# First phase of a decoder kernel: x in whole 4 KB pieces three pairs ahead, rotation tables kept in the down matrix's place, query weights behind x

## The chip, the cores and the metric

The kernel runs on one core of a Trainium2 chip. The metric is the device time of one execution in microseconds, as the median of several runs. PE is the matrix engine, DVE the vector engine, ACT the scalar engine, POOL the general engine; SP only issues transfers.

## What is computed

x and a context are [16, 256, 512], float32. Three residual steps:

```
x = x + attention(layernorm(x))          # 16 heads of 32, one shared key and value head
x = x + wkv(keys = layernorm(x), values = context)     # a recurrence over the 256 steps
x = x + ffn(layernorm(x))                # gate, up, down with ternary weights, 8-bit activations
```

What makes a first phase necessary: in the attention K and V pass through a low-rank squeeze and are then quantised to 8 bits with the minimum and maximum over **all** batches,

```
K = rope(x @ wk.T) @ k_compress.T @ k_decompress.T ;  V = x @ wv.T @ v_compress.T @ v_decompress.T
q = clip(round((t - t.min()) / ((t.max() - t.min()) / 255)), 0, 255)       # t = K, and t = V
```

so no batch's attention can start before all 16 batches' keys and values are known. Queries are rotated (rope) and attend in windows of 128 with step 64, with a normalised sigmoid. In the ffn each of the three weight matrices (4 MB) is divided by the mean of its absolute values over the whole matrix and rounded to -1, 0, 1.

## The kernel before

Activations lie in HBM twice: `x` by rows, and `xT` transposed by the host, both [16, ...] per batch. Weights come transposed too.

**First phase**, over 8 pairs of batches (j). `sync_program` loads x of the pair (`load_x`, L260, one DMA of 512 KB a batch, in pieces of 2 KB) into one of two buffers, and xT (`load_columns`, pieces of 1 KB) into one of three. DVE takes row statistics (`keys_stats`), POOL the inverse deviations (`row_rstd`), PE projects xT with the centred key and value weights (`keys_project`, L429), spreads the deviations over partitions by transposing (`keys_spread`, L440), DVE multiplies the spread deviations with the rotation table (`keys_rope`, L905, into `rope_rows`, two buffers) and the projection with that (L912); PE then applies the low-rank matrices (`keys_grow`, L449 and L456). ACT copies the raw keys and values out and stores them to HBM scratch (`keep_raw`), DVE keeps the extremes (`keys_ext`, L917). SP stores the cosine and sine rows to scratch too (`store_trig`, L272), two pairs behind the loads and in the same in-order queue; DVE's next write of that buffer waits for the store. A load of x waits until the statistics of two pairs earlier are done, a load of columns for the projection three pairs earlier. The query weights `wq_sb` are loaded at pair 3, their column means taken by PE at pair 6 (L464), and DVE centres them there (`queries_centre`, L898). After pair 7 `set_grid` takes the extremes over all partitions, with a POOL reduction.

**Between.** SP's order after the last pair's loads: queries of batch 0, its keys, its residual rows, the stores of the last two pairs' tables, four chunks of gate weights into `work` (`load_weights`, L279), the context. ACT sums each chunk's absolute values (`sum_weights`, L685, `junk` is its discarded result); after the fourth, DVE and POOL make the mean (`weight_mean`, `weight_total`).

**The loop** is a software pipeline over the batches written out by hand: iteration i does the attention of batch i, the wkv step and ffn of earlier ones. In iteration 0 DVE's order is: `keys_grid(0)`, `rope(0, 0)`, `rope(0, 1)` (L1023), `weight_mean(GATE)`, `rotate(0, 0)` (L1029), then the gate rounding (`round_weights`) and `rotate(0, 1)`. `rope` waits for PE's query products (L494, two halves), `rotate` for a transfer that swaps neighbouring rows (`turn_queries`, L319); PE's scores (L513) wait for `rotate`, and ACT's sigmoid (L722) for those. Up and down weights are loaded, summed and rounded in iterations 0 to 2, each into the chunk of `work` that the one before has left.

Of the kernel before, what the change touches and what calls it, by code (L numbers as in the profile page):

```python
# [12 lines left out]
I = 2048  # L13
# [26 lines left out]
def build(nc, a, out, k_scratch, v_scratch):  # L40

    def sb(name, shape, dt=fp32):
# [4 lines left out]
    ident_bf = sb("ident_bf", [P, P], bf16)  # L47
# [101 lines left out]
    rope_rows = [small(3 * HD, 2 * S).rearrange("p (u s) -> p u s", u=2) for k in both]  # L149
    k_raw = [small(HD, 2 * S).rearrange("p (u n) -> p u n", u=2) for k in both]  # L150

    raw = [small(P, 2 * 2 * NT * HD).rearrange("p (g n e) -> p g n e", g=2, n=2 * NT) for k in both]
    v_raw = [raw[k][:, 1].rearrange("p (u t) e -> p u t e", u=2) for k in both]
# [4 lines left out]
    squeeze_T, grow_k, grow_v = small(2 * MLA, 3 * HD), small(2 * MLA, HD), small(2 * MLA, HD)  # L158
# [7 lines left out]

    def w_chunk(m, k):
        return work[:, k * I:(k + 1) * I]
# [18 lines left out]
    first_loads, large_loads = event("first_loads", 6, 16), event("large_loads", 2, 16)  # L187
    const_loads = event("const_loads", 5, 16)
    x_loaded = [[event(f"x_loaded{k}{u}", unit=16) for u in both] for k in both]
    x_in_loaded = [event(f"x_in_loaded{k}", 2, 16) for k in range(3)]  # L190
    trig_stored = [event(f"trig_stored{k}", 2, 16) for k in both]
    kv_stored = [event(f"kv_stored{k}", 3, 16) for k in both]
# [62 lines left out]
    def sync_program(sy):  # L255

        def load_x(j, u):
            if j >= 2:
                sy.wait_ge(key_bn.sem, key_bn.at(j - 2))
            sy.dma_start(x_in[j % 2][:, u], a["x"][2 * j + u].rearrange("(t p) d -> p t d", p=P)).then_inc(  # L260
                x_loaded[j % 2][u].sem, 16)

        def load_columns(j, u):
            if j >= 3:
                sy.wait_ge(key_kv.sem, key_kv.at(j - 3))
            sy.dma_start(xT_in[j % 3][:, u], a["xT"][2 * j + u].rearrange("(c p) s -> p c s", p=P)).then_inc(
                x_in_loaded[j % 3].sem, 16)

        def store_trig(j):
            sy.wait_ge(key_rows.sem, key_rows.at(j))  # L270
            for u in both:
                sy.dma_start(k_scratch[2 * j + u, :, S:].rearrange("e (n s) -> n e s", n=2),  # L272
                             rope_rows[j % 2][0:2 * HD, u, :]).then_inc(trig_stored[j % 2].sem, 16)

        def load_weights(m, k):
            if m:
                sy.wait_ge(w_tern[m - 1].sem, w_tern[m - 1].at(0, k))
            dst = w_chunk(m, k)
            sy.dma_start(dst.rearrange("p (c n) -> p c n", n=D) if m == DOWN else dst, mats[m][k]).then_inc(  # L279
                w_loaded[m][k].sem, 16)  # L280

        def load_residual(b):
            if b == 0:
                sy.wait_ge(key_bn.sem, key_bn.at(PAIRS - 2))
            if b >= 3:
                for t in range(NT):
                    sy.wait_ge(out_stored[t].sem, out_stored[t].at(b - 3))
            sy.dma_start(x_rows[b % 3], a["x"][b].rearrange("(t p) d -> p t d", p=P)).then_inc(res_loaded[b % 2].sem, 16)

        def load_queries(b):  # L290
            if b:
                sy.wait_ge(rotated.sem, rotated.at(b - 1))
            sy.dma_start(xT, a["xT"][b].rearrange("(c p) s -> p c s", p=P)).then_inc(xT_loaded.sem, 16)

        def load_keys(b):
            if b:
                sy.wait_ge(k_set.sem, k_set.at(b - 1))
                sy.wait_ge(v_set.sem, v_set.at(b - 1))
                sy.wait_ge(roped.sem, roped.at(b - 1))
            pair = b // 2  # L300
            sy.wait_ge(kv_stored[pair % 2].sem, kv_stored[pair % 2].at(pair // 2))
            sy.wait_ge(trig_stored[pair % 2].sem, trig_stored[pair % 2].at(pair // 2))
            sy.dma_start(kv_b[:, NW * HD:], k_scratch[b].unsqueeze(0).to_broadcast([QUAD, HD, 3 * S])).then_inc(
                kv_loaded.sem, 16)
# [52 lines left out]
        for j in range(PAIRS):  # L357
            for u in both:
                load_x(j, u)
                load_columns(j, u)  # L360
            if j >= 2:
                store_trig(j - 2)
            if j == 3:
                sy.dma_start(wq_sb[:, :, :], a["wqT"].rearrange("(c p) n -> p c n", p=P)).then_inc(wq_loaded.sem, 16)
        load_queries(0)
        load_keys(0)
        load_residual(0)
        for j in (PAIRS - 2, PAIRS - 1):
            store_trig(j)
        for k in range(NC):  # L370
            load_weights(GATE, k)
# [48 lines left out]
    def tensor_program(te):  # L420
# [13 lines left out]
        def keys_spread(j):  # L434
            st, mv, rs = stats["x"]
            te.wait_ge(key_rstd.sem, key_rstd.at(j))
            if j >= 2:
# [35 lines left out]
        for j in range(PAIRS + 1):  # L473
# [7 lines left out]
            if j == PAIRS - 2:  # L481
# [174 lines left out]
    def scalar_program(se):  # L656

        se.dma_start(wkv_sb, a["wkvT"].rearrange("(c p) n -> p c n", p=P)).then_inc(first_loads.sem, 16)
        for dst, src in ((squeeze_T, "squeeze_T"), (grow_k, "grow_k"), (grow_v, "grow_v"), (ident[:, :], "ident"),
                         (rope_kv, "rope_kv")):  # L660
            se.dma_start(dst, a[src]).then_inc(first_loads.sem, 16)

        def keep_raw(j):
            if j >= 2:
                se.wait_ge(kv_stored[j % 2].sem, kv_stored[j % 2].at(j // 2 - 1))
                se.wait_ge(key_ext.sem, key_ext.at(j - 2))
            se.wait_ge(key_grown.sem, key_grown.at(j, 0))
            se.copy(k_raw[j % 2], in_bank(6, 2)[0:HD]).then_inc(key_raw.sem, 1)
            se.wait_ge(key_raw.sem, key_raw.at(j, 0))
            se.dma_start(k_scratch[2 * j:2 * j + 2, :, 0:S].rearrange("u p n -> p u n"), k_raw[j % 2]).then_inc(  # L670
                kv_stored[j % 2].sem, 16)
            se.wait_ge(key_grown.sem, key_grown.at(j, 1))
            grown = bank[TOK_BANK[j % 2]][:, 0:4 * 2 * HD].rearrange("p (n g e) -> p g n e", n=4, g=2)
            se.copy(raw[j % 2], grown).then_inc(key_raw.sem, 1)
            se.wait_ge(key_raw.sem, key_raw.at(j))
            for u in both:
                se.dma_start(v_scratch[2 * j + u].rearrange("(t p) e -> p t e", p=P), v_raw[j % 2][:, u]).then_inc(
                    kv_stored[j % 2].sem, 16)
# [34 lines left out]
        def probs(b, c):  # L713
            for j in range(QUAD):
                if b and c == 0 and j == 0:
                    se.wait_ge(num_made.sem, num_made.at(b - 1))
                elif c == 0 and j == 0:
                    for k in both:
                        se.wait_ge(trig_stored[k].sem, trig_stored[k].at(PAIRS // 2 - 1))
                        se.wait_ge(kv_stored[k].sem, kv_stored[k].at(PAIRS // 2 - 1))  # L720
# [146 lines left out]
    def vector_program(ve):  # L867
# [6 lines left out]
        def keys_stats(j):  # L874
            st, mv, rs = stats["x"]
            if j:
                ve.wait_ge(key_mv.sem, key_mv.at(j - 1))
            for u in both:
                ve.wait_ge(x_loaded[j % 2][u].sem, x_loaded[j % 2][u].at(j // 2))
                for t in range(NT):  # L880
                    ve.bn_stats(st[:, NT * u + t, :], x_in[j % 2][:, u, t, :]).then_inc(key_bn.sem, 1)
# [19 lines left out]
        def keys_rope(j):  # L901
            ve.wait_ge(key_spread.sem, key_spread.at(j))
            if j >= 2:
                ve.wait_ge(trig_stored[j % 2].sem, trig_stored[j % 2].at(j // 2 - 1))
            ve.tensor_tensor(rope_rows[j % 2], in_bank(2 + j % 2, 2)[0:3 * HD],  # L905
# [6 lines left out]
            ve.tensor_tensor(roped_kv[j % 2], in_bank(4 + j % 2, 2)[0:3 * HD], rope_rows[j % 2], op=ALU.mult).then_inc(  # L912
                key_roped.sem, 1)

        def keys_ext(j):
            ve.wait_ge(key_raw.sem, key_raw.at(j))
            ve.tensor_reduce(ext[:, :, 0, 4 * j:4 * j + 4], raw[j % 2], AX.X, ALU.max).then_inc(key_ext.sem, 1)  # L917
            ve.tensor_reduce(ext[:, :, 1, 4 * j:4 * j + 4], raw[j % 2], AX.X, ALU.min, negate=True).then_inc(
                key_ext.sem, 1)

        def round_weights(m, k):
# [7 lines left out]
            ve.wait_ge(w_bound[m].sem, w_bound[m].at(0, k))  # L929
            ve.tensor_scalar(tern_dst[m][:, k, :], w_chunk(m, k), MAGIC, None, ALU.subtract).then_inc(  # L930
# [49 lines left out]
        for j in range(PAIRS + 1):  # L980
# [8 lines left out]
            if j == PAIRS - 2:  # L989
                queries_centre()  # L990
# [306 lines left out]
    def pool_program(ge):  # L1297
        for dst, src in ((ident_bf, "ident_bf"), (blend, "blend"), (wu, "wu")):
# [130 lines left out]
def tables():  # L1429
# [11 lines left out]
        "ident_bf": np.eye(P).astype(mybir.dt.np(bf16)),  # L1441
# [43 lines left out]
```

## Time and profile before

| | us |
|---|---|
| median of 3 runs (1102.84 to 1103.45) | 1103.22 |
| the profiled execution's own time | 1107.51 |
| its span, first to last instruction | 1106.2 |
| busy PE / DVE / ACT / POOL | 860 / 848 / 707 / 437 |

Times of instructions are counted from the span's start. PE and DVE are busy 78% and 77% of the span. "Slices" are 40 equal parts of it, 27.7 us each; the first phase and iteration 0 fill the first five. In the transfers' digits 9 is 90% or more of the 16 DMA engines busy; the clock column is the share of the full TensorE clock (2.4 GHz) that was granted.

### The profile page before, as it was taken

What the parts mean: (1) busy time and instruction counts of PE and PEld (TensorE: products, weight loads), DVE (VectorE), ACT (ScalarE), POOL (GpSimd) and SP (SyncE); (2) the same over time, 40 slices, a digit from 0 to 9 for tenths busy, and PEclk for the clock granted to TensorE, in tenths of its full rate; (3) what the DMA queues carried; (4) which work ended last, traced back from release to release, by engine and by line L of the source; (5) the groups of instructions that cost most, each with busy time, mean ns of one, the idle gap of its engine ahead of it and who ended that gap; (6) DMA issues with size and microseconds to landing.
All of it is one profiled execution on the core that took longest, in us unless ns stands there. A gap on an engine that the chain in (4) does not pass through costs nothing.

```text
span 1106.2 us, 21992 instructions
## 1 busy us (share of the span) xinstructions
PE 860.3 (78%) x8301; PEld 512.9 (46%) x8388; DVE 848.1 (77%) x1630; ACT 706.9 (64%) x1179; POOL 436.7 (39%) x495
## 2 busy tenths in 40 slices
PE   5782565768888889897988888888888888986655
PEld 2341444444455555555545555555555554543222
DVE  4552659798888888888888888888788888887953
ACT  0113838077777777777768686868586868594633
POOL 2110113225353535353535354544444444445532
PEclk9896786769999999999999999999999999998978
DMA  8867516011524252525242424243342525122132
GB/s 293 288 217 277 188 58 189 10 59 36 93 68 83 78 83 78 84 78 83 79 83 78 80 82 77 85 75 87 62 99 58 104 58 103 49 78 29 39 58 66
DMA packets 148762, 106.93 MB, mean 97 GB/s; under 512 B 99792, under 2 KB 126128, under 8 KB 147504
## 3 DMA queue, kind: packets, MB, share of 16 engines
q1 hardware_dynamic: 142128, 101.48, 36.2%
q0 software_dynamic: 656, 2.63, 0.7%
q10 hardware_dynamic: 5872, 1.42, 0.6%
q8 instruction: 66, 1.08, 0.4%
q14 instruction: 40, 0.33, 0.1%
HBM read 65.65 MB, written 10.49 MB: 69 GB/s over the span
## 4 chain that ended last, share of the span: by engine, by line
ACT 31%; PE 23%; DVE 18%; issue 15%; DMA 3%; SPq 2%; POOL 1%; DVEq 0%; ACTq 0%; POOLq 0%
PE bank L494 9%; ACT arena L722 6%; PE bank L593 5%; PE bank L513 5%; ACT L774 3%; ACT sums L729 3%; DVE junk L1146 3%; PE bank L583 2%; ACT sums L734 2%; ACT junk L774 2%; ACT junk L779 2%; DVE amax L1112 2%; DVE fs L1155 2%; ACT L745 2%; ACT L722 2%
## 5 line engine op out<-in xcount | busy, mean ns | idle before, releaser
L583 PE MATMUL bank<-w_up_gate,qT 128*128 128x512 bf16 x966 | 232.5, 386 | 48.4 <-ACT junk L774 24.1
L1350 POOL TENSOR_TENSOR work<-junk,lnw 128x512 f32<-128x512 f32 x128 | 188.2, 1490 | 125.1 <-DVE junk L1146 110.7
L1333 POOL TENSOR_TENSOR sums<-sums,blend 128x448 f32<-128x448 f32 x64 | 73.2, 1163 | 270.5 <-ACT sums L734 270.5
L583 PEld LDWEIGHTS bank<-w_up_gate,qT 128*128 128x128 bf16 x1024 | 96.5, 99 | 155.3 <-ACT junk L774 26.9
L593 PE MATMUL bank<-w_down,work 128*128 128x512 bf16 x483 | 125.6, 408 | 25.3 <-ACT junk L774 10.6
L494 PE MATMUL bank<-wide,wq_sb 128*128 128x256 f32 x512 | 117.7, 389 | 27.7 <-DVE rows L1047 27.7
L513 PE MATMUL bank<-wide,k_win 32*128 32x128 f32 x1536 | 70.5, 320 | 82.2 <-ACT arena L722 54.2
L722 ACT ACTIVATE arena<-bank 128x384 f32<-128x384 f32 x256 | 104.8, 496 | 36.7 <-PE bank L513 36.6
L494 PEld LDWEIGHTS bank<-wide,wq_sb 128*128 128x128 f32 x512 | 98.3, 195 | 53.1 <-issue 39.7
L774 ACT ACTIVATE junk<-bank,deq 128x512 f32<-128x512 f32 x128 | 86.3, 686 | 52.5 <-PE bank L583 50.7
L545 PE MATMUL bank<-wo_sb,wide 128*128 128x512 f32 x256 | 115.9, 607 | 4.1 <-DVE wide L1040 4.1
L1146 DVE TENSOR_TENSOR junk<-bank,junk 128x512 f32<-128x512 f32 x128 | 87.7, 685 | 28.4 <-PE bank L583 18.7
L513 PEld LDWEIGHTS bank<-wide,k_win 32*128 32x128 f32 x1536 | 56.7, 213 | 106.4 <-ACT arena L722 71.9
L758 ACT ACTIVATE work<-work,fs 128x2048 f32<-128x2048 f32 x32 | 63.9, 1996 | 58.8 <-DVE fs L1168 58.8
L1068 DVE TENSOR_TENSOR_SCAN sums<-wkv_s,sums 128x256 f32<-128x256 f32 x128 | 98.6, 838 | 0.0
L779 ACT ACTIVATE junk<-junk 128x512 f32<-128x512 f32 x128 | 80.7, 631 | 20.9 <-DVE junk L1146 20.8
L593 PEld LDWEIGHTS bank<-w_down,work 128*128 128x128 bf16 x512 | 48.3, 103 | 88.4 <-issue 25.6
L545 PEld LDWEIGHTS bank<-wo_sb,wide 128*128 128x128 f32 x256 | 49.7, 195 | 62.0 <-issue 55.7
L1155 DVE TENSOR_REDUCE fs<-work 128x1 f32<-128x2048 f32 x32 | 72.8, 2276 | 0.4 <-POOL work L1350 0.4
L1023 DVE TENSOR_TENSOR wide<-bank,kv_b 128x512 f32<-128x512 f32 x64 | 41.0, 683 | 39.8 <-PE bank L555 38.5
L752 ACT ACTIVATE wide<-wide,amax 128x512 f32<-128x512 f32 x32 | 21.4, 714 | 78.4 <-DVE amax L1124 78.4
L524 PE MATMUL bank<-arena,v_win 128*32 128x128 f32 x1536 | 55.6, 278 | 9.2 <-ACT sums L729 7.5
(150 smaller groups left out, 1541.2 us busy)
## 6 DMA issues: line engine op xcount, KB each, us to landing
rows<-in_x SPq DMA_DIRECT2D x24, 512.0 KB, 5.4
sums<-in_xT SPq DMA_DIRECT2D x16, 512.0 KB, 8.8
wide<-in_xT SPq DMA_DIRECT2D x16, 512.0 KB, 4.2
ctx_T<-in_ctxT SPq DMA_DIRECT2D x16, 512.0 KB, 4.0
wide<-wide SPq DMA_DIRECT2D x64, 128.0 KB, 2.1
out<-rows SPq DMA_DIRECT2D x32, 256.0 KB, 2.2
kv_b<-k_raw SPq DMA_DIRECT2D x16, 384.0 KB
wide<-in_x SPq DMA_DIRECT2D x8, 512.0 KB, 9.3
```

What stands on the lines that cost most here:

```text
L494: last = te.matmul(in_bank(k, 2)[:, n % 2, :], wq_sb[:, c, n * P:(n + 1) * P], xT[:, c, :], start=c == 0, stop=c == NC - 1)
L513: last = te.matmul(bank[j][:, n * P:(n + 1) * P], k_win[head, window], q_cos[head, c, window], start=True, stop=True, skip_group_check=True)
L545: last = te.matmul(bank[t][:, :], heads_T[:, c, t * P:(t + 1) * P], wo_sb[:, c, :], start=c == 0, stop=c == NC - 1)
L583: last = te.matmul(bank[4 + k % 4][:, :], qT[:, c, t * P:(t + 1) * P], w_up_gate[:, m, c, cols], start=c == 0, stop=c == NC - 1)
L593: last = te.matmul(bank[6 + t][:, :], hid_T[:, t, c, :], w_down[:, c, :], start=c == 0, stop=c == NI - 1)
L722: se.activation(prob[:, :, QUAD * c + j, :], bank[j][:, 0:NW * P].rearrange("p (k q) -> p k q", k=NW), ACT.Sigmoid, scale=float(1.0 / np.s ...
L774: se.activation(gated[:, n % 2, :], bank[4 + 2 * (n % 2)][:, :], ACT.Silu, scale=deq[:, 0, t:t + 1]).then_inc(silu_set.sem, 1)
L779: se.activation(gated[:, n % 2, :], hid[:, n % 2, :], ACT.Square, accum_out=fs[:, t, n:n + 1]).then_inc(sq_set.sem, 1)
L1068: ve.tensor_tensor_scan(state[:, c, n, 1:S + 1], sc["decay"][:, c:c + 1].to_broadcast([P, S]), GG[:, c, n, :], 0.0, ALU.mult, ALU.add).the ...
L1146: ve.tensor_tensor(hid[:, n % 2, :], bank[4 + k % 4][:, :], gated[:, n % 2, :], op=ALU.mult).then_inc(hid_set.sem, 1)
L1155: ve.tensor_reduce(col[t]["am"], hid_w[:, t, :], AX.X, ALU.max, apply_absolute_value=True).then_inc(h_peak.sem, 1)
L1350: ge.tensor_tensor(hid_w[:, t, cols], hid[:, n % 2, :], lnw[:, cols], op=ALU.mult).then_inc(z_set.sem, 1)
```

## The change

- x and xT (and the context) are laid out by the host so that each partition's part is one run of 4 KB; one DMA of 1 MB loads a pair's x, another its columns. The loop's loads use the same layout.
- x has three buffers; the third is chunk 2 of `work`. So gate chunk 2 waits for the statistics of pair 5.
- `rope_rows` has one place for every pair, in the memory of `w_down`; its stores go out three pairs behind, and the last three are placed between later loads. The down rounding waits for all of them.
- raw keys and values have four buffers in place of two; a pair's values are stored by one DMA.
- `wq` is loaded after all x, its means are taken at pair 7 ahead of that pair's `keys_grow`, and centred inside `set_grid`. The gate chunks are issued before the last three table stores, residual and context after them. `wo` and `lnw` are issued after the gate weights' total.
- PE's first work waits for two small loads in place of six (three of them joined into one, two with their own event); SP waits for those two after issuing pair 0. The unused `ident_bf` goes.

```diff
+    def w_chunk(m, k):
+        return work[:, k * I:(k + 1) * I]
-    x_in = [rows[:, 0:2], wide[:, 1:3, :].rearrange("p u (t d) -> p u t d", t=NT)]
+    x_in = [home.rearrange("p (u t d) -> p u t d", u=2, t=NT) for home in
+            (rows[:, 0:2].rearrange("p k t d -> p (k t d)"), wide[:, 1:3, :].rearrange("p k n -> p (k n)"),
+             w_chunk(0, 2))]
+    rope_rows = [w_down[0:3 * HD].rearrange("p c n -> p (c n)").bitcast(fp32)[:, j * 2 * S:(j + 1) * 2 * S].rearrange(
+        "p (u s) -> p u s", u=2) for j in range(B // 2)]
...
-        def load_x(j, u):
-            if j >= 2:
-                sy.wait_ge(key_bn.sem, key_bn.at(j - 2))
-            sy.dma_start(x_in[j % 2][:, u], a["x"][2 * j + u].rearrange("(t p) d -> p t d", p=P)).then_inc(
-                x_loaded[j % 2][u].sem, 16)
+        def load_x(j):
+            if j >= 3:
+                sy.wait_ge(key_bn.sem, key_bn.at(j - 3))
+            sy.dma_start(x_in[j % 3].rearrange("p u t d -> p u (t d)"), a["x"][2 * j:2 * j + 2].rearrange(
+                "u p n -> p u n")).then_inc(x_loaded[j % 3].sem, 16)
...
         def store_trig(j):
             sy.wait_ge(key_rows.sem, key_rows.at(j))
+            if j >= 4:
+                sy.wait_ge(trig_stored[j % 4].sem, trig_stored[j % 4].at(j // 4 - 1))
...
         def load_weights(m, k):
             if m:
                 sy.wait_ge(w_tern[m - 1].sem, w_tern[m - 1].at(0, k))
+            elif k == 2:
+                sy.wait_ge(key_bn.sem, key_bn.at(5))
...
         for j in range(PAIRS):
-            for u in both:
-                load_x(j, u)
-                load_columns(j, u)
-            if j >= 2:
-                store_trig(j - 2)
-            if j == 3:
-                sy.dma_start(wq_sb[:, :, :], a["wqT"].rearrange("(c p) n -> p c n", p=P)).then_inc(wq_loaded.sem, 16)
+            load_x(j)
+            load_columns(j)
+            if j == 0:
+                sy.wait_ge(first_loads.sem, first_loads.at(0))
+            if j >= 3:
+                store_trig(j - 3)
+        sy.dma_start(wq_sb[:, :, :], a["wqT"].rearrange("(c p) n -> p c n", p=P)).then_inc(wq_loaded.sem, 16)
         load_queries(0)
         load_keys(0)
+        load_weights(GATE, 0)
+        load_weights(GATE, 1)
+        store_trig(5)
+        load_weights(GATE, 2)
+        load_weights(GATE, 3)
+        store_trig(6)
         load_residual(0)
-        for j in (PAIRS - 2, PAIRS - 1):
-            store_trig(j)
-        for k in range(NC):
-            load_weights(GATE, k)
+        store_trig(7)
         load_values(0)
...
-            if j == PAIRS - 2:
+            if j == PAIRS - 1:
                 te.wait_ge(wq_loaded.sem, wq_loaded.at(0))
                 column_means(bank[0][:, :], wq_sb, wq_mean)
...
             ve.wait_ge(key_ext.sem, key_ext.at(PAIRS - 1))
             ve.tensor_reduce(ext1[:, :], ext[:, :, :, :].rearrange("p g m n -> p (g m) n"), AX.X, ALU.max).then_inc(ext_col.sem, 1)
+            queries_centre()
             ve.wait_ge(ext_everywhere.sem, ext_everywhere.at(0))
...
+        weight_total(GATE)
         ge.dma_start(wo_sb[:, :, :], a["woT"].rearrange("(c p) n -> p c n", p=P)).then_inc(large_loads.sem, 16)
         ge.dma_start(lnw[:, :], a["lnw"].to_broadcast([P, I])).then_inc(large_loads.sem, 16)
-        ge.wait_ge(key_kv.sem, key_kv.at(PAIRS - 1))
-        weight_total(GATE)
```

## Rows read from the trace of the kernel before

**Rows 1.** The page's transfers, by slices of 27.7 us, in tenths
```profile
DMA  8867516011524252525242424243342525122132
```
**Rows 2.** Chain of waits that ended last: start us, us, what
```profile
84.26 18.14 DMA work<-in_wgT
...
106.21 1.90 ACT junk L685 x2
...
108.13 0.17 DVE abs_sum L957
...
109.18 0.68 DVE wide L1029
...
110.00 1.71 PE bank L513 x24
```
**Rows 3.** Stretches: length, busy us of PE, PEld, DVE, ACT, POOL, clock, DMA share, GB/s
```profile
2.00:14.00 12.00, 2.10 (x9) 1.96 (x10) 0.07 (x1) 1.28 (x1) 2.27 (x5) 1.00 1.03 328
34.00:42.00 8.00, 6.12 (x22) 2.79 (x22) 4.35 (x19) 1.25 (x4) 1.21 (x2) 1.00 1.06 365
66.00:82.00 16.00, 15.43 (x61) 7.85 (x60) 9.62 (x20) 2.84 (x6) 1.21 (x2) 1.00 0.54 154
90.00:98.00 8.00, 0.00 (x0) 0.00 (x0) 0.00 (x0) 0.80 (x1) 0.00 (x0) 0.63 1.02 424
151.00:153.00 2.00, 2.00 (x11) 1.77 (x10) 0.81 (x5) 0.00 (x0) 0.94 (x2) 1.00 1.03 397
106.00:126.00 20.00, 8.95 (x144) 7.62 (x148) 16.66 (x19) 12.89 (x23) 0.40 (x1) 0.50 0.52 153
```
**Rows 4.** Waits of the engines, 0 to 100 us: total us, times, longest
```profile
DVE stats_x L881 <- DMA wide<-in_x: 10.1, 6, 2.3
...
DVE stats_x L881 <- DMA rows<-in_x: 9.1, 5, 3.3
...
PE bank L429 <- DMA sums<-in_xT: 9.1, 3, 5.4
```
**Rows 5.** Waits of SP's queue, 0 to 200 us
```profile
SPq L260 <- DVE stats_x L881: 19.7, 10, 9.8
```
**Rows 6.** PE in order of time, 14 to 29 us: start, us, what
```profile
14.63 6.47 PE L429 MATMUL bank<-sums,arena 128*96 128x512 f32 x8
...
21.38 3.60 PE L429 MATMUL bank<-sums,arena 128*96 128x512 f32 x8
...
27.26 1.91 PE L429 MATMUL bank<-sums,arena 128*96 128x512 f32 x4
```
**Rows 7.** Instructions in order of time, 60 to 180 us
```profile
68.94 3.65 PE L464 MATMUL bank<-wq_sb,arena 128*128 128x512 f32 x8
...
72.43 3.60 PE L429 MATMUL bank<-sums,arena 128*96 128x512 f32 x8
...
73.86 2.27 DVE L898 TENSOR_TENSOR wq_sb<-wq_sb,bank 128x2048 f32<-128x2048 f32 x1
...
80.93 7.13 PE L494 MATMUL bank<-wide,wq_sb 128*128 128x256 f32 x32
...
82.34 0.29 DVE L967 TENSOR_REDUCE ext<-ext 128x4 f32<-128x128 f32 x1
...
88.17 1.29 DVE L1023 TENSOR_TENSOR wide<-bank,kv_b 128x512 f32<-128x512 f32 x2 [1.30 <-PE bank L494]
...
110.00 1.66 PE L513 MATMUL bank<-wide,k_win 32*128 32x128 f32 x24 [21.94 <-DVE wide L1029]
```
**Rows 8.** The page's transfers by line: KB each, us from issue to landing
```profile
wide<-wide SPq DMA_DIRECT2D x64, 128.0 KB, 2.1
...
arena<-in_wkvT ACTq DMA_DIRECT2D x1, 192.0 KB, 4.6
```
**Rows 9.** Waits in the loop, 300 to 1000 us
```profile
PE bank L494 <- DVE rows L1047: 20.1, 12, 1.9
```
**Rows 10.** PE in order of time in the loop, 330 to 365 us
```profile
344.08 0.95 PE L513 MATMUL bank<-wide,k_win 32*128 32x128 f32 x24
```

More of the change, by code:

```diff
@@ L46, in build @@
     ident = sb("ident", [P, P])
-    ident_bf = sb("ident_bf", [P, P], bf16)
     blend = sb("blend", [P, OUTS])
@@ L148, in build @@
     roped_kv = [small(3 * HD, 2 * S).rearrange("p (u s) -> p u s", u=2) for k in both]
[L149 to L153, printed above, removed]
+    k_raw = [small(HD, 2 * S).rearrange("p (u n) -> p u n", u=2) for k in range(4)]
+    raw = [small(P, 2 * 2 * NT * HD).rearrange("p (g n e) -> p g n e", g=2, n=2 * NT) for k in range(4)]
+    v_raw = [raw[k][:, 1] for k in range(4)]
     wkv_sb = small(P, NC * 3 * HD).rearrange("p (c n) -> p c n", c=NC)
@@ L157, in build @@
     grown_by = small(3 * HD, 2 * HD)
-    squeeze_T, grow_k, grow_v = small(2 * MLA, 3 * HD), small(2 * MLA, HD), small(2 * MLA, HD)
+    low_rank = small(2 * MLA, 5 * HD)
+    squeeze_T, grow_k, grow_v = low_rank[:, 0:3 * HD], low_rank[:, 3 * HD:4 * HD], low_rank[:, 4 * HD:]
     mats = [a["wgT"].rearrange("(c p) n -> c p n", p=P), a["wuT"].rearrange("(c p) n -> c p n", p=P),
@@ L184, in event @@
         return Event(nc, name, per, unit)
[L187 to L192, printed above, removed]
+    first_loads, table_loads, large_loads = event("first_loads", 2, 16), event("table_loads", 2, 16), event("large_loads", 2, 16)
+    const_loads = event("const_loads", 4, 16)
+    x_loaded = [event(f"x_loaded{k}", unit=16) for k in range(3)]
+    x_in_loaded = [event(f"x_in_loaded{k}", unit=16) for k in range(3)]
+    trig_stored = [event(f"trig_stored{k}", 2, 16) for k in range(4)]
+    kv_stored = [event(f"kv_stored{k}", 2, 16) for k in range(4)]
     w_loaded = [[event(f"w_loaded{m}{k}", unit=16) for k in range(NC)] for m in range(3)]
@@ L300, in load_keys @@
             pair = b // 2
-            sy.wait_ge(kv_stored[pair % 2].sem, kv_stored[pair % 2].at(pair // 2))
-            sy.wait_ge(trig_stored[pair % 2].sem, trig_stored[pair % 2].at(pair // 2))
+            sy.wait_ge(kv_stored[pair % 4].sem, kv_stored[pair % 4].at(pair // 4))
+            sy.wait_ge(trig_stored[pair % 4].sem, trig_stored[pair % 4].at(pair // 4))
             sy.dma_start(kv_b[:, NW * HD:], k_scratch[b].unsqueeze(0).to_broadcast([QUAD, HD, 3 * S])).then_inc(
@@ L658, in scalar_program @@
         se.dma_start(wkv_sb, a["wkvT"].rearrange("(c p) n -> p c n", p=P)).then_inc(first_loads.sem, 16)
-        for dst, src in ((squeeze_T, "squeeze_T"), (grow_k, "grow_k"), (grow_v, "grow_v"), (ident[:, :], "ident"),
-                         (rope_kv, "rope_kv")):
-            se.dma_start(dst, a[src]).then_inc(first_loads.sem, 16)
+        se.dma_start(low_rank, a["low_rank"]).then_inc(first_loads.sem, 16)
+        for dst, src in ((ident[:, :], "ident"), (rope_kv, "rope_kv")):
+            se.dma_start(dst, a[src]).then_inc(table_loads.sem, 16)
         def keep_raw(j):
-            if j >= 2:
-                se.wait_ge(kv_stored[j % 2].sem, kv_stored[j % 2].at(j // 2 - 1))
-                se.wait_ge(key_ext.sem, key_ext.at(j - 2))
+            if j >= 4:
+                se.wait_ge(kv_stored[j % 4].sem, kv_stored[j % 4].at(j // 4 - 1))
+                se.wait_ge(key_ext.sem, key_ext.at(j - 4))
             se.wait_ge(key_grown.sem, key_grown.at(j, 0))
-            se.copy(k_raw[j % 2], in_bank(6, 2)[0:HD]).then_inc(key_raw.sem, 1)
+            se.copy(k_raw[j % 4], in_bank(6, 2)[0:HD]).then_inc(key_raw.sem, 1)
             se.wait_ge(key_raw.sem, key_raw.at(j, 0))
-            se.dma_start(k_scratch[2 * j:2 * j + 2, :, 0:S].rearrange("u p n -> p u n"), k_raw[j % 2]).then_inc(
-                kv_stored[j % 2].sem, 16)
+            se.dma_start(k_scratch[2 * j:2 * j + 2, :, 0:S].rearrange("u p n -> p u n"), k_raw[j % 4]).then_inc(
+                kv_stored[j % 4].sem, 16)
             se.wait_ge(key_grown.sem, key_grown.at(j, 1))
             grown = bank[TOK_BANK[j % 2]][:, 0:4 * 2 * HD].rearrange("p (n g e) -> p g n e", n=4, g=2)
-            se.copy(raw[j % 2], grown).then_inc(key_raw.sem, 1)
+            se.copy(raw[j % 4], grown).then_inc(key_raw.sem, 1)
             se.wait_ge(key_raw.sem, key_raw.at(j))
-            for u in both:
-                se.dma_start(v_scratch[2 * j + u].rearrange("(t p) e -> p t e", p=P), v_raw[j % 2][:, u]).then_inc(
-                    kv_stored[j % 2].sem, 16)
+            se.dma_start(v_scratch[2 * j:2 * j + 2].rearrange("u (t p) e -> p (u t) e", p=P), v_raw[j % 4]).then_inc(
+                kv_stored[j % 4].sem, 16)
         def sum_weights(m, k):
@@ L717, in probs @@
                 elif c == 0 and j == 0:
-                    for k in both:
-                        se.wait_ge(trig_stored[k].sem, trig_stored[k].at(PAIRS // 2 - 1))
-                        se.wait_ge(kv_stored[k].sem, kv_stored[k].at(PAIRS // 2 - 1))
+                    for stored in kv_stored:
+                        se.wait_ge(stored.sem, stored.at(1))
                 se.wait_ge(scored.sem, scored.at(b, QUAD * c + j))
@@ L929, in round_weights @@
             ve.wait_ge(w_bound[m].sem, w_bound[m].at(0, k))
+            if m == DOWN and k == 0:
+                for trig in trig_stored:
+                    ve.wait_ge(trig.sem, trig.at(1))
             ve.tensor_scalar(tern_dst[m][:, k, :], w_chunk(m, k), MAGIC, None, ALU.subtract).then_inc(
@@ L1297, in pool_program @@
     def pool_program(ge):
-        for dst, src in ((ident_bf, "ident_bf"), (blend, "blend"), (wu, "wu")):
+        for dst, src in ((blend, "blend"), (wu, "wu")):
             ge.dma_start(dst.ap(), a[src]).then_inc(const_loads.sem, 16)
```

44 lines of the change are left out of this document (22 added, 22 removed).

## The prediction

> **What bounds the kernel now.** I read the slices of the page first: the DMA digits are 8, 8, 6, 7 in the first four slices of 27.7 us and mostly 2 to 5 after the seventh, so transfers can only bind in the first phase and in the first two iterations of the loop [rows 1]. The chain of waits then shows what ends that stretch: from 84.26 to 102.40 us it lies on the gate weights' transfer, then on ACT's sums of them, the mean on DVE and POOL, and at 109.18 on L1029, the first rotate, from which PE's scores of batch 0 start at 110.00 [rows 2]. Everything later (scores, probabilities, up weights) hangs on this rotate, so I take **109.2 us** as the mark and ask when it comes after the change.
>
> The stretches show why it is late [rows 3]. At 34 to 42 us, the x pairs streaming, the DMA is full at 365 GB/s; at 66 to 82 it is half empty (0.54, 154 GB/s) and yet the gate weights, which need nothing of the first phase, are issued only at its end; at 90 to 98 they stream at 424 GB/s with PE and DVE at rest. In the waits of the first 100 us DVE and PE stood about 19 and 9 us for x [rows 4], while SP stood 19.7 us for DVE's statistics to free an x buffer [rows 5]: two buffers only, and rotation stores in the same queue. So the first phase has two faults: transfers that start late, and 4.2 MB of weights behind all.
>
> In the loop proper the query products wait for DVE's residual (20.1 us over 12 batches) and for no transfer [rows 9], so faster loads of x, queries and context there are worth 0; without that cover they would be worth at most their own fraction of a microsecond an iteration.
>
> **The change part by part.** Times are of the profiled execution (span 1106.2, its own time 1107.5 us); the median of the runs is 1103.2, 4.3 less, and I subtract the same difference.
>
> *a) Start.* PE now waits for two small loads and not for six: wkvT lands 4.6 us after its issue at 0.7 [rows 8], the low-rank tile, small and right behind it, at about 6 (estimate). Its first 3 us of work then lie beside the landing of x pair 0. Up to xT of pair 0 some 3.0 MB come (2.1 of x, 0.36 on ACT's queue, 0.5 on POOL's); at 328 GB/s, the rate of 2 to 14 us [rows 3], and 2 us of start, that is 11.0. The first projection took 6.47 us at the slow level against 3.6 later [rows 6], so pair 1 starts at about 17.5, against 21.38. SP's new wait for the first loads holds pair 1's loads until about 6; the 3.0 MB before them last to 11, which covers it. If it held them to 12, the phase would slip 1 us.
>
> *b) Pace of a pair.* PE needs 27.26 - 21.38 = 5.9 us for project, spread and grow at the full clock [rows 6]; from 17.5 six more pairs bring the last projection to **53** at best. DVE has time over: it stood 19 us in this phase for x alone [rows 4]. By the DMA: 16.8 MB of x and xT, 0.9 of constants, 0.65 of rotation stores, 0.8 of raw keys and values up to then, 19.1 MB. At 365 GB/s [rows 3] that is 52.3, plus 2 of start: **54.3**. What 4 KB pieces bring has no row of its own. Bounds: nothing, or even the first rate, 328: 60.2; all of it, the weights' 424: 47, where PE's 53 binds. The stores and the 128-byte values remain, so I stay at the mixed 365 and take **T7 = 55**, range 53 to 60. Before, pair 7's projection started at 72.43 [rows 7].
>
> The rule that speaks against this part is in the Trainium skill, DMA: Bandwidth & Descriptors, Specifications: a transfer reaches line rate from 512 bytes on. By it 1 KB and 2 KB pieces are as good as 4 KB. The down weights in 2 KB pieces at 397 [rows 3] agree with it; the 328 and 365 of x do not, unless the other traffic makes them. By the rule T7 is what the old rate gives, 54 to 60, which is my range anyway.
>
> *c) The deeper buffers, whole loads, tables in w_down.* Fewer issues, no store between DVE and its rows, raw buffers four deep: what they bring is that the DMA stays fed, already counted in b. SP's new waits (store j-4 for store j, statistics 5 for gate chunk 2) are for events a pair or more old; behind them in the queue stand the loads of x j+1 at most, and three pairs of cover are 18 us. Below nothing is excluded only by that cover; with it gone a wait would cost the 1.7 us of two store issues. DVE's wait in the down rounding is for stores over 100 us old: 0. The missing identity, joined value stores: 0.
>
> *d) From the last projection to the mark.* This is a new bound, since the query weights are centred only after the extremes. From T7: projection, spread, grow of pair 6, 5.9; column means of wq 3.65; grow of pair 7, 2.0: 11.6. From PE's end to that of the last extreme on DVE, with ACT's copy and two reductions between, 80.93 to 82.63: 1.7, so 13.3. Centring 2.3: 15.6. It was hidden at 73.86 and stands on the path now. Queries 7.1 (first half 3.6, at 19.2; second at 22.7) [rows 7]. Rope of the first half 1.3: 20.5, its turn 0.5 of issue and 2.1 of landing [rows 8]: 23.1. Rope of the second: 24.0. The mean of the gate weights 1.05 (108.13 to 109.18, [rows 2]): 25.05. The mark is at 55 + 25.1 = **80.1**. Where a step waits for a colleague's queue I have put 0; 1 us of such slips is in the range.
>
> *e) The gate weights.* They must be summed by 79.0. After xT7 (55) come wq 1.05, queries 0.5, keys 0.45, gate 4.2, stores 0.5: 6.7 MB, at 424 GB/s 16 us: landed at 71. Three sums of 2.0 after ACT's last copy (67.5) [rows 2] are done at 73.6, set_keys follows, then the fourth until 77.5. Slack 1.5 us; it is the next thing to be late. The query weights land at 55 + 0.5 + 2.5 + 1 = 59, needed at 61.
>
> *f) wo and lnw* (2.1 MB) now come after the weights' total, beside the up weights: 5 us of DMA at 424 GB/s. They cover the time in which DVE rounds the first gate chunk, and ACT comes to the up sums only after three groups of scores and probabilities, at least 10 us past the mark: 0, at most 2 lost.
>
> *g) Clock.* PE stood 21.9 us up to its first scores [rows 7] and worked at the lower level, 0.50 of 2.4 GHz, from 106 to 126 [rows 3]: a group of 24 score products took 1.7 us there [rows 7] and 0.95 at the full level [rows 10]. Now PE would stand only about 3 us before it. Four groups on the chain at 0.7 give 2.8; nothing if the clock falls anyway. I take half, **1.4**.
>
> **Sum:** 109.2 - 80.1 + 1.4 = **30.5 us**; 1107.5 - 30.5 = 1077.0 profiled, **1073** as a median. Own range: T7 53 and the full 2.8 of the clock give 1069.
>
> **The rivals.**
> *R1, the pieces bring nothing and the old pace of the full DMA is the slow one.* For it: 328 at the start though nothing else ran; against: 365 later with stores in between. At 328, T7 = 60.2, the mark 85.3; with the clock's 1.4 as before, 1103.2 - 23.9 - 1.4 = **1078**. The skill's 512-byte rule above would give this number. 0.17.
> *R2, the gate weights stay the bound, or contention gives back.* SP's queue is in order: if store 5 or 6, or a full ring (the 18 us on the gate weights in [rows 2] show how long a crowded queue takes), puts the last chunk at 78, sum and mean bring the mark to 83 to 85; or wo and lnw put 2 us on the up sums. 3 to 6 less: **1078**. 0.15.
> *R3, it doesn't do what it says:* the loads still drip, since a buffer is freed by DVE and PE that themselves wait, as in [rows 4, 5]. Then only the 9 us of PE's waits and 4 of the weights' head start come: **1090**. 0.08.
> *R4, slower: PE at the lower clock through the first phase.* Its place is the pair's 5.9 us, its price 3.6 to 6.47 for a projection and the like for the rest, some 10.5 a pair. From 17.5, T7 = 17.5 + 6 x 10.5 = 80.5; the 18.7 us of PE's work in d take 15 more: mark 120.6, 11.4 later than before, **1115**. It decides once PE is slow in that tail and in three of the six pairs (each 4.6; 29.1 - 15 = 14). Against: in the stretches the clock is 1.00 while x streams and below it only where PE had stood [rows 3], and now it stands less. 0.04.
>
> **How the numbers follow.** Forecast (1069 to 1077) 0.55, R1 0.17, R2 0.15, R3 0.08, R4 0.04, and 0.01 for no change. Within 0.2% (2.2 us) is what a measurement of this kernel cannot tell from no change. Range: from 1068 to 1087, which takes in R1 and R2 and the bounds of b, leaves most of R3 and R4 out.
>
> **What would show it.** Pair 7's projection at 53 to 60 and the DMA near 1.0 up to there; the gate weights landed by 76 with DVE's grid at 71 to 73; L898 after the last extremes; the first rotate at 79 to 86; the scores' groups at 1.7 or 0.95; the distance from the rotate to the end as before (997 us) less 1 to 3. The forecast is wrong if PE's projections wait for xT beyond pair 1 by more than 1 us each, if ACT waits for the gate weights after its copies, or if the distance from the mark to the end grows.

## The result, and the profile after

The changed kernel takes 1099.25 us (median of 7 runs, 1095.6 to 1100.2) against 1103.45 (7 runs, 1102.1 to 1107.7): ratio 0.9949, 95% interval 0.9930 to 0.9968. It is faster by 0.5%, where 2.7% was forecast; the range, 1068 to 1087, doesn't hold it.

By slices, the first phase is no denser than before (against [rows 1]):

```profile
DMA  8876424020515151515142524242424343212022
```

The stretches, columns as in [rows 3], show that it starts well and then falls off: 0.97 of the DMA engines at 22 to 42 us, 0.76 at 42 to 62, while PE waits.

```profile
22.00:42.00 20.00, 20.00 (x73) 8.95 (x72) 16.40 (x48) 3.14 (x8) 4.15 (x7) 1.00 0.97 360
34.00:42.00 8.00, 8.00 (x28) 3.49 (x27) 6.28 (x22) 1.25 (x4) 1.21 (x2) 1.00 0.91 305
42.00:62.00 20.00, 16.71 (x59) 7.52 (x57) 11.03 (x29) 2.52 (x6) 2.41 (x4) 0.91 0.76 251
```

In order of time (start, us, engine, line, what, and in brackets what it waited for), from pair 6's projection to the mark of the prediction, the first rotate (L1043 now). These answer to [rows 7]:

```profile
54.09 5.37 PE L441 MATMUL bank<-sums,arena 128*96 128x512 f32 x8 [2.40 <-DMA sums<-in_xT]
...
63.00 3.67 PE L441 MATMUL bank<-sums,arena 128*96 128x512 f32 x8 [1.09 <-DMA sums<-in_xT]
...
69.20 3.70 PE L478 MATMUL bank<-wq_sb,arena 128*128 128x512 f32 x8
...
76.34 2.28 DVE L910 TENSOR_TENSOR wq_sb<-wq_sb,bank 128x2048 f32<-128x2048 f32 x1
...
78.88 10.14 PE L508 MATMUL bank<-wide,wq_sb 128*128 128x256 f32 x32 [3.96 <-DVE wq_sb L910]
...
89.13 1.29 DVE L1037 TENSOR_TENSOR wide<-bank,kv_b 128x512 f32<-128x512 f32 x2 [2.17 <-PE bank L508]
...
94.24 0.16 DVE L972 TENSOR_REDUCE abs_sum<-abs_sums 128x1 f32<-128x4 f32 x1 [3.83 <-ACT junk L698]
...
101.16 0.69 DVE L1043 TENSOR_TENSOR wide<-wide 128x512 f32<-128x512 f32 x1 [5.87 <-DMA wide<-wide]
```

Pair 7's projection starts at 63.0 (72.4 before), the mark is at 101.2 (109.2). The span fell by 7.4 us, the mark by 8.0: the whole gain lies ahead of it. SP's queue shows what the phase suffered from; each row is a DMA issue, its second number the time SP spent on it:

```profile
11.24 0.37 SPq L265 DMA_DIRECT2D wide<-in_x  x1
...
37.75 4.70 SPq L265 DMA_DIRECT2D rows<-in_x  x1
...
54.52 5.37 SPq L373 DMA_DIRECT2D wq_sb<-in_wqT  x1
...
66.20 6.71 SPq L279 DMA_DIRECT2D k_raw<-w_down  x2
...
72.96 8.51 SPq L288 DMA_DIRECT2D work<-in_wgT  x2
...
92.44 2.48 SPq L328 DMA_DIRECT2D wide<-wide  x4
```

A load of x that took 0.4 us to issue takes 4.2 to 4.7 from 29 us on (one of columns 0.8 to 1.3), and SP runs back to back until 92. So the queries' swap (`turn_queries`), due at 87 when the first half is roped, goes out at 92.4. Yet the DMA engines are not full: their share is 0.76 at 42 to 62 us. The trace also records each DMA engine's completion of a transfer. For two loads of x, the first table stores, and the swap (completions in us):

```
x of pair 6:      14 engines 46.76 to 46.93, the last two 51.14 and 51.40
x of pair 7:      14 engines 54.74 to 54.95, the last two 60.36 and 60.39
tables of pair 0: first store 29.97 30.20, second 31.53 31.89 (issued 21.9 to 23.1)
swap, first half: 28 of 32 (two DMAs) 95.19 to 96.47, the last four 99.23 99.56 99.97 101.14
```

A table store has two such completions (and one event at the end of its own issue), so it ran on two engines. The loads of x of pairs 0 to 3, issued ahead of the first stores, complete together; from pair 4 on each waits 3.0 to 5.4 us for the last two of its sixteen.

The kernel before shows the same. The stretch "DMA work<-in_wgT" of [rows 2] is its third gate chunk, issued at 84.26 us: 14 completions come by 96.98, the last two at 101.08 and 102.40. Of the first chunk 14 come by 88.43, the last two at 96.19 and 97.17. So part of what the prediction read as the time of the weights' bytes was two engines too.

### The profile page after: what moved, and what is told of

Read it like the earlier page. It is cut to its first block, busy times and chain, and to the rows that moved or that the text cites. A ratio compares the mean times of both kernels' runs of the same rounds, so it can differ in the third digit from the quotient of the medians.

```text
span 1098.8 us, 22051 instructions
## 1 busy us (share of the span) xinstructions
PE 878.8 (80%) x8388; PEld 516.9 (47%) x8388; DVE 844.1 (77%) x1630; ACT 706.2 (64%) x1179; POOL 435.7 (40%) x494
## 4 chain that ended last, share of the span: by engine, by line
ACT 30%; PE 26%; DVE 20%; issue 15%; SPq 5%; DMA 2%; POOL 2%; DVEq 0%; ACTq 0%; POOLq 0%
PE bank L508 9%; ACT arena L734 6%; PE bank L607 5%; PE bank L527 4%; ACT L786 3%; ACT sums L741 3%; DVE junk L1160 3%; PE bank L597 3%; ACT sums L746 2%; ACT junk L786 2%; ACT junk L791 2%; DVE amax L1126 2%; DVE fs L1169 2%; ACT L757 2%; ACT L734 2%
## 5 line engine op out<-in xcount | busy, mean ns | idle before, releaser
L597 PE MATMUL bank<-w_up_gate,qT 128*128 128x512 bf16 x1024 | 244.9, 389 | 40.4 <-ACT junk L786 20.6
L508 PE MATMUL bank<-wide,wq_sb 128*128 128x256 f32 x512 | 120.8, 397 | 34.8 <-DVE rows L1061 30.8
L607 PE MATMUL bank<-w_down,work 128*128 128x512 bf16 x512 | 132.0, 408 | 19.8 <-ACT junk L786 10.5
L508 PEld LDWEIGHTS bank<-wide,wq_sb 128*128 128x128 f32 x512 | 100.6, 199 | 61.2 <-issue 46.9
L607 PEld LDWEIGHTS bank<-w_down,work 128*128 128x128 bf16 x512 | 48.0, 103 | 87.0 <-issue 23.1
L559 PEld LDWEIGHTS bank<-wo_sb,wide 128*128 128x128 f32 x256 | 49.8, 195 | 60.5 <-issue 55.6
## 6 DMA issues: line engine op xcount, KB each, us to landing
sums<-in_xT SPq DMA_DIRECT2D x8, 1024.0 KB, 11.2
```

Of the source, the lines that this page charges most:

```text
L508: last = te.matmul(in_bank(k, 2)[:, n % 2, :], wq_sb[:, c, n * P:(n + 1) * P], xT[:, c, :], start=c == 0, stop=c == NC - 1)
L559: last = te.matmul(bank[t][:, :], heads_T[:, c, t * P:(t + 1) * P], wo_sb[:, c, :], start=c == 0, stop=c == NC - 1)
L597: last = te.matmul(bank[4 + k % 4][:, :], qT[:, c, t * P:(t + 1) * P], w_up_gate[:, m, c, cols], start=c == 0, stop=c == NC - 1)
L607: last = te.matmul(bank[6 + t][:, :], hid_T[:, t, c, :], w_down[:, c, :], start=c == 0, stop=c == NI - 1)
```

## The experiments

All times are medians with the ratio to the kernel before on the same chip. "Mark" is the first rotate on DVE, T7 the start of pair 7's projection.

**1. The table stores spread over the engines.** On the changed kernel:

```diff
-            for u in both:
-                sy.dma_start(k_scratch[2 * j + u, :, S:].rearrange("e (n s) -> n e s", n=2),
-                             rope_rows[j][0:2 * HD, u, :]).then_inc(trig_stored[j % 4].sem, 16)
+            for n in both:
+                sy.dma_start(k_scratch[2 * j:2 * j + 2, :, (1 + n) * S:(2 + n) * S].rearrange("u e s -> e u s"),
+                             rope_rows[j][n * HD:(n + 1) * HD]).then_inc(trig_stored[j % 4].sem, 16)
```

> The changed kernel, with one edit: the rotation tables' two stores of a pair are cut by table (cosine, sine) with 32 rows outermost, and not by batch with the two tables outermost. Same bytes, same pieces of 1 KB, same count of DMAs. In the changed kernel's trace 14 of 16 completions of an x load come within 0.2 us and the last two 3 to 5 us later (46.9 and 51.4 us for pair 6), and a table store shows completions from 2 engines. Theory A (the stores sit on two engines, whose queues hold up every load behind them, and through the full queues SP's issues): the late completions vanish, PE keeps 5.9 us a pair, pair 7's projection starts at 56 to 58 (63.0 now), the first rotate comes at 80 to 88 (101.2 now), time 1078 to 1088 us. Theory B (SP's issuing itself is slow, 1 to 5 us for a load whatever the engines do): issues stay back to back, pair 7 at 61 or later, rotate within 3 us of 101, time 1096 to 1100. Theory C (HBM delivers no more with stores beside): as B for the times, but the 16 completions come together.

Measured: 1082.0 us, ratio 0.9798 (0.9776 to 0.9820). Stretches, PE and SP of its trace:

```profile
22.00:42.00 20.00, 20.00 (x76) 9.13 (x75) 18.18 (x52) 3.15 (x8) 3.85 (x7) 1.00 1.04 407
42.00:62.00 20.00, 20.00 (x77) 9.36 (x77) 13.45 (x38) 3.67 (x8) 3.62 (x6) 1.00 1.06 368
```
```profile
49.71 3.62 PE L441 MATMUL bank<-sums,arena 128*96 128x512 f32 x8
...
55.62 3.62 PE L441 MATMUL bank<-sums,arena 128*96 128x512 f32 x8
...
71.16 9.69 PE L508 MATMUL bank<-wide,wq_sb 128*128 128x256 f32 x32 [3.97 <-DVE wq_sb L910]
...
84.42 1.67 PE L527 MATMUL bank<-wide,k_win 32*128 32x128 f32 x24 [3.57 <-DVE wide L1043]
```
```profile
31.73 0.53 SPq L265 DMA_DIRECT2D rows<-in_x  x1
...
43.94 0.50 SPq L373 DMA_DIRECT2D wq_sb<-in_wqT  x1
...
80.94 2.45 SPq L328 DMA_DIRECT2D wide<-wide  x4
```

Theory A holds: PE is busy throughout at 5.9 us a pair, T7 is 55.6 (0.4 before its range), the mark 83.6. The issues of x take 0.4 to 0.5 us, the sixteen completions of pair 6's x lie within 1.1 us (43.26 to 44.37), and a store now has sixteen. B and C are out: neither the issues nor HBM were slow of themselves. The same bytes in the same 1 KB pieces cost 17 us by where they were sent.

**2. The spread alone, on the kernel before** (the same edit with its two buffers).

> The kernel before, with the stores' spread alone and nothing else of the change. Theory A: here too two engines lag, but the stores of the last pairs and the gate weights still come at the end, so part of the gain only: pair 7's projection at 64 to 69 (72.4 before), first rotate at 98 to 105 (109.2), time 1093 to 1100 us. Theory B or C: no change, 1102 to 1105.

Measured: 1091.6 us, ratio 0.9872 (0.9848 to 0.9895), better than A's range and than the whole change without it. From its chain of waits:

```profile
66.71 3.43 PE bank L429 x8
...
75.61 8.26 PE bank L494 x32
...
84.51 10.11 DMA wide<-wide
94.62 0.02 issue
94.64 0.70 DVE wide L1029
```

T7 is 66.7 and the mark 94.6, 3.4 us before my range: I had put the gate weights as the last to arrive, but ACT has summed all four by 90.3, and the swap, issued behind them into the same queue (10.1 us to land), comes last.

**3. Without SP's wait for the first small loads**, on experiment 1:

```diff
-            if j == 0:
-                sy.wait_ge(first_loads.sem, first_loads.at(0))
```

> The changed kernel with the spread stores, and without SP's wait for the first two small loads after pair 0. In the changed kernel pair 1's loads are issued at 11.2 us, and the DMA is 0.83 busy from 2 to 14. If the wait costs: 1 to 3 us less than the kernel with the spread stores alone. If PE's pace (5.9 a pair) binds from pair 1 on: same within 1 us. If the wait is worth its price (small loads land sooner by it): the first column means start 1 to 5 us later than 11.4 and the time is 1 to 4 us more.

Measured: 1083.0 us, ratio 0.9795 (0.9779 to 0.9812), no difference from experiment 1. The DMA is 0.97 busy from 2 to 14 us in place of 0.79, but the first column means come at 11.9 (11.6 with the wait), pair 7 starts at 56.7 and not at 55.6, and PE's pace binds. In the time the wait neither costs nor brings anything that can be told.

**4. The query weights early again**, on experiment 1:

```diff
-        sy.dma_start(wq_sb[:, :, :], ...)              # after the last pair's loads
+            if j == 5:
+                sy.dma_start(wq_sb[:, :, :], ...)
-            if j == PAIRS - 1:                         # PE, column means
+            if j == PAIRS - 2:
-            queries_centre()                           # in set_grid
+            if j == PAIRS - 2:
+                queries_centre()                       # in DVE's loop over the pairs
```

> The kernel with the spread stores (1082.0 us), and the query weights again early: loaded after pair 5's loads, their column means at pair 6, centred there and not after the extremes. In the trace of the spread stores PE stands 4.0 us (67.2 to 71.2) while DVE centres, and its query products then take 9.7 us and not the 7.1 they take elsewhere, at a lower granted clock. Theory (the centring behind the extremes is a new bound, dearer than its own 2.3 us since PE cools): products start at 66 to 68 at 7.1, both halves roped by 76, the first rotate at 77 to 80 (83.6 with the spread stores), time 1075 to 1079 us. Rival (the extra 1 MB ahead of the last pairs holds x by its 2.6 us, or the gate weights bind at once): rotate at 81 or later, 1080 to 1083.

Measured: 1078.9 us, ratio 0.9760 (0.9734 to 0.9786). PE and DVE of its trace:

```profile
68.20 7.13 PE L509 MATMUL bank<-wide,wq_sb 128*128 128x256 f32 x32
```
```profile
78.64 0.16 DVE L973 TENSOR_REDUCE abs_sum<-abs_sums 128x1 f32<-128x4 f32 x1 [1.92 <-ACT junk L699]
...
79.61 0.67 DVE L1045 TENSOR_TENSOR wide<-wide 128x512 f32<-128x512 f32 x1
...
113.34 0.16 DVE L973 TENSOR_REDUCE abs_sum<-abs_sums 128x1 f32<-128x4 f32 x1 [0.92 <-ACT junk L699]
```

The mark moved by 4.0 us to where the theory put it, 79.6. The products end 5.5 us earlier: 3.0 by their earlier start, 2.6 by their pace (7.13 in place of 9.69 us; the granted clock is 1.00 from 68 to 76 us, where experiment 1 has 0.73 from 71 to 81), and PE no longer stands 4 us before them. The mark gains less, since now the mean of the gate weights comes last and waits for ACT's sums (1.92 us, first line of DVE), not for a transfer: ACT starts on them right behind its copies. Of the 4.0 us 2.5 are left in the span (1080.2 and 1077.7), and the time's interval overlaps that of experiment 1, so the 3 us in the medians stand on the traces more than on the times.

**5. wo and lnw ahead of the gate total**, on experiment 1 (POOL's two `dma_start` moved one line up, before `weight_total(GATE)`).

> The kernel with the spread stores (1082.0 us), and POOL's two large loads (wo, lnw, 2.1 MB) issued right after the extremes' reduction, ahead of the gate weights' total, and not behind it. With the spread stores the chain waits from 92.7 to 106.9 for up weights, and from the first rotate to the up weights' sum on DVE (L972) it is 34.2 us, against 31.2 before the change. Theory (the two loads crowd out the up weights): that distance falls to 31 to 32, time 1078 to 1080. Rival (the up weights are late for another reason, such as the keys' load beside them): no change, 1081 to 1083; if the two loads hold the gate weights instead: first rotate later than 83.6 by 1 to 3, 1083 to 1085.

Measured: 1080.4 us, ratio 0.9767 (0.9735 to 0.9800). From the mark (84.60) to the mean of the up weights (115.80) it is 31.2 us in place of 34.2 (33.3 and 33.2 in experiments 3 and 7, with both loads in the old place too):

```profile
84.60 0.69 DVE L1043 TENSOR_TENSOR wide<-wide 128x512 f32<-128x512 f32 x1 [0.41 <-DMA wide<-wide]
...
115.80 0.16 DVE L972 TENSOR_REDUCE abs_sum<-abs_sums 128x1 f32<-128x4 f32 x1 [0.91 <-ACT junk L698]
```

ACT's wait of 2.1 us for an up chunk is gone, so the mechanism is shown, worth 2 to 3 us of that distance. The mark itself is 1.0 later than in experiment 1; experiment 3, with both loads in the old place, has it at 85.0, so the traces differ by as much of themselves. The gain in the time (1.6 us) isn't clear of its interval.

**6. Both.**

> Both edits together on the spread stores: if they are independent, 1082 - 5 - 3 = 1072 to 1076 us. If the gate weights bind once the centring is gone, the two loads in front of them cost 1 to 3: 1075 to 1079, and ACT waits for the gate weights before its sums.

Measured: 1081.8 us, ratio 0.9785 (0.9758 to 0.9812), worse than either expected, and by a third way:

```profile
84.43 0.69 DVE L1045 TENSOR_TENSOR wide<-wide 128x512 f32<-128x512 f32 x1 [4.59 <-DMA wide<-wide]
```

ACT doesn't wait for the gate weights. It is the queries' swap, 128 KB a DMA, that is late: issued at 75.6, with the products 3 us earlier and faster, it completes at 79.7 to 84.4, while wo and lnw, issued at 70.5 and 71.4, complete at 76.9 to 83.0. In experiment 5, where the swap goes out at 81.9, it lands in 2 us. I had counted only the two users I had been looking at.

**7. The old pieces**, on experiment 1: x, xT and context in the host layouts of before (2 KB and 1 KB), a pair still in one DMA.

```diff
-            sy.dma_start(... a["xT"][2 * j:2 * j + 2].rearrange("u p n -> p u n"))
+            sy.dma_start(... a["xT"][2 * j:2 * j + 2].rearrange("u (c p) s -> p (u c) s", p=P))
...                                                # the same for x, and for the loop's loads
```

> The kernel with the spread stores (1082.0 us), but x, xT and the context in the old layouts, 2 KB and 1 KB a piece, still whole pairs in one DMA and three buffers. The full DMA moved 407 GB/s from 22 to 42 us with 4 KB pieces and spread stores, 374 with the old pieces in the kernel before with spread stores. Theory (pieces of 4 KB move faster): 350 to 380 there, pair 7's projection 3 to 5 us later than 55.8, time 1084 to 1088. Rival (from 512 bytes on all pieces are alike, the old layouts cost nothing, and the old 374 came from late issues): 400 or more, 1081 to 1083.

Measured: 1084.1 us, ratio 0.9803 (0.9774 to 0.9833).

```profile
22.00:42.00 20.00, 19.76 (x75) 8.97 (x74) 17.25 (x50) 3.29 (x9) 3.62 (x6) 1.00 1.09 376
```
```profile
8.48 1.99 PE L478 MATMUL bank<-arena 128*128 128x96 f32 x8 [8.48 <-DMA arena<-in_low_rank]
...
55.95 3.67 PE L441 MATMUL bank<-sums,arena 128*96 128x512 f32 x8
```

The rate is the theory's (376 against 407 GB/s), T7 the rival's, 0.3 us later. But that is a sum of two: pair 1 starts at 18.5, 1.7 us earlier than in experiment 1, and six pairs then take 37.4 us in place of 35.4, with short waits for columns. The earlier start comes from the small loads. The 10 KB low-rank load lands 7.1 us after its issue and not 10.2, so PE's first work starts at 8.5 and not at 11.6. So the 4 KB pieces bring 8% of the full DMA's rate, 2.0 us over six pairs, and cost 1.7 at the start. In the median nothing can be told (ratios 0.9803 and 0.9798).

**8. The keys' load spread**, on experiment 4, **and 9. wo and lnw late**, on 8. A batch's keys go to four groups of 32 partitions as one DMA with the copies outermost, and its completions come from 4 engines.

```diff
-            sy.dma_start(kv_b[:, NW * HD:], k_scratch[b].unsqueeze(0).to_broadcast([QUAD, HD, 3 * S])).then_inc(
-                kv_loaded.sem, 16)
+            for q in range(QUAD):
+                sy.dma_start(kv_b[q * HD:(q + 1) * HD, NW * HD:], k_scratch[b]).then_inc(kv_loaded.sem, 16)
```

> The kernel with spread stores and early query weights (1078.9 us), with the load of a batch's keys and tables (384 KB, four copies over the partitions) cut into four DMAs of one copy each. As one DMA it shows completions from 4 engines only, so these four carry 96 KB each while the up weights stand behind them in the same queues. Theory (uneven loads hold the up weights too): ACT's wait of 2.1 us for an up chunk goes, the distance from the first rotate to the up weights' mean falls from 33.7 to 31 to 32, time 1075 to 1078 us. Rival (the wait is wo's and lnw's bytes, as the run with early wo suggests): within 1 us of 1078.9; three more issues of 0.5 us an iteration on SP cost nothing, since SP rests in the loop, or 1 to 2 us if they hold the swap of the queries.

Measured: 1076.3 us, ratio 0.9733 (0.9714 to 0.9752). The time is in the theory's range, the mechanism only in part. The second up chunk no longer has four late engines (all sixteen from 98.69 to 100.50; in experiment 4 twelve by 97.44 and four from 101.78 to 102.47), and ACT's wait for it is gone. But ACT now waits 1.9 us for the first chunk, and mark to mean is still 33.5 us (81.43 to 114.96). Nor does the trace show a gain in time: it is of the slowest of the four executions (1079.6 us, experiment 4's 1079.0), with a mark 1.8 later than there, since pair 6's projection, after a wait of 1.2 us for its columns, took 5.4 us in place of 3.7. What gave the lower median, if anything, stays open; its interval overlaps that of experiment 4.

In 9 SP issues wo and lnw behind `load_weights(UP, 3)`.

> The same, and wo and lnw issued by SP behind the last up chunk instead of by POOL before the first. Early they stood in front of the queries' swap (4.6 us of wait in the run with both edits), in their old place in front of the up weights. Theory: first rotate stays at 79 to 80, the distance to the up weights' mean is 31 to 32, and wo, needed some 30 us after the rotate, lands at 20 to 24: 1074 to 1077 us. If wo comes too late PE waits before the first output product, and the time is 1 to 4 more than that of the kernel beside it.

Measured: 1075.9 us, ratio 0.9729 (0.9709 to 0.9749), the fastest kernel of the study.

```profile
79.76 0.67 DVE L1047 TENSOR_TENSOR wide<-wide 128x512 f32<-128x512 f32 x1
...
111.24 0.16 DVE L975 TENSOR_REDUCE abs_sum<-abs_sums 128x1 f32<-128x4 f32 x1 [0.91 <-ACT junk L701]
```

Mark at 79.8 and 31.5 us from there, with no wait of ACT for an up chunk: both loads are out of both users' way, as the theory has it. In the medians it can't be told from 8.

## Why the prediction was wrong

The forecast for the span was 1075.7, measured 1098.8: 23.1 us. By its steps:

- **b, the pace: the step that failed.** "19.1 MB at 365 GB/s" took the sixteen engines as one pipe. 8.0 us of the miss are here (T7 at 63.0, forecast 55). The bytes were right; the 64 KB of each table store lay on two engines, and every load behind them in the queue is done only when its slowest engine is. An estimate from the rows: of a pair's 2 MB each engine carries 128 KB, and these two carry 64 KB of tables besides. At 407 GB/s over sixteen engines (experiment 1) that is 7.7 us a pair and not 5.2, more than PE's 5.9; the last four projections start 6.9, 8.5 and 8.9 us apart. The trace of before held a hint that I passed over: SP spent from 1.2 to 5.3 us on the pairs' stores there, and the share of 1.06 at 34 to 42 us [rows 3] fell to 0.80 in the next 20 us, which I put down to buffers not yet free.
- That experiment 1 gives T7 = 55.6, nearly the 55 of the forecast, is luck in the number. The forecast had the DMA set it, with PE free to reach 53. In experiment 1 PE sets it, at 5.9 us a pair from a start at 20.2, and the DMA moves 407 GB/s, not 365.
- **d and e, the tail:** 38.2 us from T7 to the mark, forecast 25.1: 13.1 of the miss. It lies in three places. PE's products took 10.1 in place of 7.1, after it had stood 4.0 us at the centring (in experiment 4 both are gone), and the first half was roped 3.5 us late. SP was stuck in its queue until 92.4, so the swap went out 5.5 us after it was due: R2's mechanism, "SP's queue is in order", which I gave 3 to 6 us. And from its first issue to the mark it was 8.7 us in place of 2.6: 28 of its 32 completions had come by 96.5, the rest, the last at 101.1, are the lagging engines once more. The forecast had left 2.0 us between the swap and the mark, and these are used up first. Experiment 1 alone brings the tail to 28.0, so some 10 of the 13 us are again the two slow engines. The 2.9 that remain are mostly the products (9.7 in place of 7.1).
- **c, the deeper buffers, "already counted in b":** what they bring alone no run shows. With the stores spread the whole rest of the change (buffers, layout, order) brings T7 from 66.7 to 55.6 and the ratio from 0.9872 to 0.9798. With the stores as they were it brings less: T7 from 72.4 to 63.0, and the ratio 0.9949.
- **a, the start:** the low-rank load landed at 11.2, not at 6, and wkvT took 9.8 us to land where the kernel before took 4.6 [rows 8]. With the old pieces of 1 and 2 KB the low-rank load landed at 8.3 (experiment 7), so 3 us of the delay are a price of the 4 KB pieces. Pair 1 started at 21.0 (forecast 17.5). In the sum this 3.5 us error doesn't show, for what set T7 was b's two engines.
- **f and g:** mark to the end 997.6, forecast 995.6. wo and lnw cost 2 to 3 us in the up weights' sums (experiment 5), and the clock gave nothing: score groups took 1.67 us, as PE had stood 13.0 us before the first. In experiment 1 it stood 3.6 us, about what g had asked for, and they took 1.67 as well (granted clock 0.50 from 84 to 100 us).
- The rule of the Trainium skill weighed in b (DMA: Bandwidth & Descriptors, Specifications), line rate from 512 bytes: the trace disagrees in rate (376 against 407 GB/s, experiment 7). In the time it can't be told.

The rule that would have told is another one of the same page. The Trainium skill, DMA: Bandwidth & Descriptors, in the section on why a DMA increments its semaphore by 16, says that a transfer is dealt to the largest number of engines up to 16 that divides the slowest dimension on both sides. The stores' outermost dimension was the 2 tables, and the trace agrees: 2 completions; the keys' load has 4 copies outermost, 4 completions; with 32 rows outermost there were 16.

The whole account: of the 30.5 us forecast, 7.4 came; spreading the stores brings 18.6 more in the span (17 in the median). The 4.5 that are still missing are 3.5 at the mark (0.6 in T7, 2.9 in the tail) and 1.0 behind it.

## What to carry to other kernels

For each DMA look at which dimension stands outermost on both sides and at how many engines complete it. Here a small store on two of sixteen engines held every load of x behind it by 3.0 to 5.4 us, and showed as slow issues and as a DMA share of 0.76 to 0.97 while PE or SP waited, not as a full DMA. Divide bytes by a rate only where the load is even, and use the share of all engines as a bound only in that case. When a transfer is moved, list everybody else who will be in the engines at its new time, the 128 KB swap as well as the weights. And when pieces are made larger, look at what small loads beside them pay.

## What the runs showed of the hardware that was not expected

- An issue of 1 MB of x on SP's queue took 0.4 to 0.5 us in experiment 1 and 4.2 to 4.7 us, from 29 us on, where two of its sixteen engines lagged. Issues of other transfers took up to 3.3 us in experiment 1 too (47.26 us), so a slow issue alone doesn't tell of lagging engines.
- The queries' products took 10.1 or 9.7 us after 4.0 us of standing (granted clock 0.73 in experiment 1) and 7.1 in experiment 4 without it. Standing isn't all: in experiment 2 they took 8.5 us, at 0.83, with no gap over 0.6 us in the 32 us before. Why is open.
- A 10 KB load issued at 1.2 us landed 10.0 us later beside 2 MB of x in pieces of 4 KB, and 7.1 us later beside the same bytes in pieces of 1 and 2 KB.
